# Grouped attention with its queries computed transposed, and the rotation's two parts stacked in 128 rows

## The reference

```
Q = (layernorm(x) @ Wq) -> 16 heads of 64      K, V = ctx @ Wk, ctx @ Wv -> 4 groups of 64
rope(x1, x2) = (x1 * c1 - x2 * s1,  x1 * s2 + x2 * c2)      # halves of 32; position = row
scores = rope(Q) . rope(K) / 8 + rel_pos_bias;  masked
x = x + softmax(scores) @ V -> heads side by side -> @ Wo
```

## Time and profile before

| | us |
|---|---|
| 3 runs, median (lowest, highest) | 1008.42 (1007.82, 1012.86) |
| the profiled execution | 1005.3 |
| its span | 1003.5 |
| TensorE matmul busy | 899.9 (90%) |
| VectorE busy | 669.8 (67%) |
| ScalarE busy | 420.8 (42%) |
| GpSimd busy | 375.3 (37%) |
| grouped attention, first query product to last output | 581.5 to 800.5 |

### The profile page before, as it was taken

The page is one execution under the profiler, slowest core; times in us unless marked ns, Lnnn a source line. Parts: engine busy times, 40 slices in busy tenths (PEclk is TensorE's granted clock), DMA queues, the critical chain, the costliest instruction groups (busy, mean ns, idle before and its releaser), DMA issues. The chain is left out here.

```text
span 1003.5 us, 17466 instructions
## 1 busy us (share of the span) xinstructions
PE 899.9 (90%) x5857; PEld 642.7 (64%) x5864; DVE 669.8 (67%) x1572; ACT 420.8 (42%) x1134; POOL 375.3 (37%) x279
## 2 busy tenths in 40 slices
PE   2899989999889995868899979999999949999997
PEld 2687744444478873744378647777777727778786
DVE  5899968889689988876377698787767531222221
ACT  2566641000146555752455336565655512122222
POOL 1776403333476732506545503333333430111111
PEclk9999999999899997987999999999999969999999
DMA  6100079999400007202356392311110149534200
GB/s 210 59 1 0 1 199 306 319 313 311 170 1 1 0 1 190 87 0 92 112 169 203 91 332 73 112 54 51 51 51 26 43 157 318 190 110 141 93 12 20
DMA packets 87259, 117.17 MB, mean 117 GB/s; under 512 B 12464, under 2 KB 75949, under 8 KB 86781
## 3 DMA queue, kind: packets, MB, share of 16 engines
q1 hardware_dynamic: 77455, 88.15, 29.1%
q10 hardware_dynamic: 4408, 15.46, 4.4%
q0 software_dynamic: 5328, 12.70, 3.5%
HBM read 68.08 MB, written 50.16 MB: 118 GB/s over the span
## 5 line engine op out<-in xcount | busy, mean ns | idle before, releaser
L1016 PE MATMUL psum<-m_W,lnT 128*128 128x512 f32 x256 | 114.2, 598 | 0.7 <-DVE acc L928 0.7
L410 POOL TENSOR_TENSOR prob<-prob,a_rden 128x1232 f32<-128x1232 f32 x30 | 67.5, 2249 | 58.4 <-DVE a_rden L506 58.4
L1016 PEld LDWEIGHTS psum<-m_W,lnT 128*128 128x128 f32 x256 | 47.2, 190 | 59.0 <-issue 56.5
L2907 ACT ACTIVATE prob<-psum,x_b 128x320 f32<-128x320 f32 x64 | 33.7, 527 | 117.1 <-PE psum L2963 117.1
L2574 PE MATMUL psum<-g_VW,pT 128*128 128x256 f32 (+1 forms) x320 | 72.5, 382 | 1.6 <-ACT pT L2461 1.5
L1001 POOL TENSOR_TENSOR m_masked<-m_rel,m_mrow 128x1232 f32<-128x1232 f32 x16 | 41.8, 2614 | 82.9 <-DMA masked_bias<-m_masked 62.0
L2769 POOL DMA_INDIRECT out_x<-x_yt,x_X x20 | 19.8, 991 | 135.3 <-DVE x_yt L2846 135.3
L2574 PEld LDWEIGHTS psum<-g_VW,pT 128*128 128x128 f32 (+1 forms) x320 | 59.5, 190 | 11.2 <-issue 3.7
L2232 POOL TENSOR_TENSOR g_qr<-g_t 128x1024 f32<-128x1024 f32 x15 | 35.4, 2359 | 71.1 <-DVE g_t L2305 71.1
L2239 POOL TENSOR_TENSOR prob<-prob,g_rden 128x1232 f32<-128x1232 f32 x15 | 33.7, 2247 | 67.6 <-DVE g_rden L2340 67.6
L2524 PE MATMUL psum<-g_Wq,lnT 128*128 128x512 f32 x128 | 58.0, 596 | 0.7 <-ACT lnT L2435 0.7
(11 more groups left out here) (464 smaller groups left out, 2235.6 us busy)
## 6 DMA issues: line engine op xcount, KB each, us to landing
routed_rows<-hole SPq DMA_DIRECT2D x8, 2210.0 KB, 33.5
masked_bias<-m_masked ACTq DMA_DIRECT2D x16, 616.0 KB, 7.5
g_bias<-masked_bias SPq DMA_DIRECT2D x16, 616.0 KB, 3.8
m_xb<-routed_rows SPq DMA_DIRECT2D x39, 130.0 KB
m_rel<-in_rel_bias ACTq DMA_DIRECT2D x8, 616.0 KB, 9.6
expert_rows<-hole SPq DMA_DIRECT2D x1, 4680.0 KB, 32.4
g_early_w<-in_L_ffn_w SPq DMA_DIRECT2D x8, 512.0 KB, 4.6
g_early_w<-in_L_ffn_w SPq DMA_DIRECT2D x4, 1024.0 KB, 5.9
```

The costliest lines, as they stand in the source:

```text
L410: nc.gpsimd.tensor_tensor(heads(c.prob[b]), heads(c.prob[b]), rden[b][:, :].unsqueeze(2).to_broadcast([P, H, SK]), ALU.mult).then_inc(norm ...
L1016: last = nt.matmul(c.ps[p][:, :], c.lnT[b][:, k * P:(k + 1) * P], W[:, k, p * 512:(p + 1) * 512], start=(k == 0), stop=(k == KC - 1))
```

## The change

The product is turned round: Wq is now the stationary side and the transposed tile the moving one, so queries arrive with the numbers of two heads on the rows and tokens on the columns. VectorE multiplies them by tables of 64 rows into `turned`, where each head has 128 rows: one half the product with the table "to itself", the other with the table "to the partner". The keys are stored once as they are and once with halves exchanged, one below the other, so one matmul of 128 rows gives a head's scores. GpSimd's sum, the 8 transposes and the 2 copies are gone; scores are 16 matmuls of 77 columns. The rotation of a tile is split around the softmax's shift.

```diff
+        def rope(i, u):
+            q = c.psall[:, q_bank(i) * 512:q_bank(i) * 512 + 1024].rearrange("p (m n) -> p m n", n=P)
+            to = turned[i % 2][:, :].rearrange("p (m u n) -> p m u n", u=2, n=P)
+            n0 = i % HALF * P
+            own, other = slice(u * DH, (u + 1) * DH), slice((1 - u) * DH, (2 - u) * DH)
+            if u == 0:
+                dve.wait_ge(s["q_ps"], i + 1)
+                wait(dve, s["s_ps"], i - 1)
+            for rows_, table in ((own, turn[0]), (other, turn[1])):
+                last = nv.tensor_tensor(to[rows_, :, u, :], q[own, :, :],
+                                        table[own, n0:n0 + P].unsqueeze(1).to_broadcast([DH, HB // 2, P]), ALU.mult)
...
+        def queries(i):
+            pe.wait_ge(s["lnT_ok"], i + 1)
+            if i >= 2:
+                pe.wait_ge(s["roped"], 1 if i == 2 else i)
+            for m in range(HB // 2):
+                to = c.psall[:, q_bank(i) * 512 + m * P:q_bank(i) * 512 + (m + 1) * P]
                 for k in range(KC):
+                    last = nt.matmul(to, Wq[:, k, m * P:(m + 1) * P], c.lnT[i % 2][:, k * P:(k + 1) * P],
+                                     start=(k == 0), stop=(k == KC - 1))
...
+        def scores(t):
+            pe.wait_ge(s["roped"], t + 1)
             wait(pe, s["s_used"], t)
+            for h in range(HB):
+                o = h // HPB * 512 + h % HPB * SK
+                last = nt.matmul(c.psall[:, o:o + SK], turned[t % 2][:, h * P:(h + 1) * P], KB[:, t // HALF, h // G, :],
+                                 start=(h % HPB == 0), stop=(h % HPB == HPB - 1 or h == HB - 1), skip_group_check=True)
```

```diff
+            nv.reduce_max(mx[b][:, halves[0]], p[:, halves[0]], AX, negate=True).then_inc(s["mx_ok"], 1)
             dve.wait_ge(s["s_used"], t + 1)
+            nv.reduce_max(mx[b][:, halves[1]], p[:, halves[1]], AX, negate=True).then_inc(s["mx_ok"], 1)
```

The orders are written anew. VectorE in step t: rope(t+1, 0), shift(t), rope(t+1, 1), the router's work, the residual of tile t-1 (`finished`), the experts' results of one or two tiles (`collect`; groups of statistics are now 0, 1-3, 4-6, 7-10, 11-15), reciprocals (`divisors`). ScalarE and TensorE:

```diff
+        deviation(0)
+        layer_norm(0)
+        lnT_copy(0)
+        deviation(1)
+        na.activation(spare[:, :], c.ones[:, 0:1], ACT.Exp)
+        for i in range(1, 4):
+            layer_norm(i)
+            lnT_copy(i)
+        for t in range(NT):
...
+            if t > 0:
+                pT_copy(t - 1, 0)
+                pT_copy(t - 1, 1)
+            if 2 <= t and t + 3 < NT:
+                layer_norm(t + 3)
+            exps(t, 0, 2)
+            if t > 0:
+                pT_copy(t - 1, 2)
+            exps(t, 2, HB // 2)
+            if t == LOGITS_AT:
+                route(t)
+            exps(t, HB // 2, HB)
...
+        lnT(0)
+        queries(0)
+        lnT(1)
+        queries(1)
+        lnT(2)
+        for t in range(NT + 1):
             banks_read(t)
+            if t < NT:
+                scores(t)
             if t == 0:
+                queries(2)
+                lnT(3)
+            if t == NT - 1:
...
+                pe.wait_ge(s["pT_ok"], (NT - 2) * 3)
+                keep_warm(c, ring[0], 6)
...
+                prob_transpose(t - 1, 0)
+                prob_transpose(t - 1, 1)
...
+                output(t - 1, 0)
+                prob_transpose(t - 1, 2)
+                if t < NT:
+                    route(t)
+                output(t - 1, 1)
+                if 2 <= t and t + 3 < NT:
+                    lnT(t + 3)
+                output(t - 1, 2)
+                back(t)
+                if t + 2 < NT:
+                    queries(t + 2)
+                if t == 1:
+                    lnT(4)
```

More of the change, by code:

```diff
@@ L2224, in _ @@
         ng = nc.gpsimd
[L2226 to L2232, removed]
+        for t in range(NT - 1):
+            b = t % 2
             if t == NT - 2:
@@ L2236, in step @@
                     scatter_tile(c, r, k)
[L2237 to L2245, removed]
+            pool.wait_ge(s["rd_ok"], t + 1)
+            ng.tensor_tensor(heads(c.prob[b]), heads(c.prob[b]),
+                             rden[b][:, :].unsqueeze(2).to_broadcast([P, HB, SK]), ALU.mult).then_inc(s["p_ok"], 1)
+        for k in range(3, HALF):
+            scatter_tile(c, r, k)
     @programs.vector
@@ L2262, in add_experts @@
                 stats = nv.bn_stats(bst_of(c, i), xt(c, tile(i)))
[L2263 removed]
+            if tiles[-1] + 1 in [hi for _, hi in NORM_GROUPS]:
                 chain(stats)
@@ L2330, in residual, with divisors @@
-        def residual(i, b):
+            nv.reduce_max(mx[b][:, halves[1]], p[:, halves[1]], AX, negate=True).then_inc(s["mx_ok"], 1)
+        def divisors(t):
+            b = t % 2
+            wait(dve, s["p_ok"], t - 1)
+            dve.wait_ge(s["exp_ok"], t + 1)
+            nv.reciprocal(rden[b][:, :], den[b][:, :]).then_inc(s["rd_ok"], 1)
+            if t == NT - 1:
+                p = heads(c.prob[b])
+                dve.wait_ge(s["rd_ok"], t + 1)
+                for h in halves:
+                    nv.tensor_tensor(p[:, h], p[:, h], rden[b][:, h].unsqueeze(2).to_broadcast([P, HB // 2, SK]),
+                                     ALU.mult).then_inc(s["p_last"], 1)
@@ L2331, in residual, with finished @@
+        def finished(i):
             dve.wait_ge(s["y_ps"], i + 1)
             nv.tensor_tensor(xt(c, tile(i)), xt(c, tile(i)), bank_y[:, 0:D], ALU.add).then_inc(s["x_ok"], 1)
[L2334 to L2344, removed]
-                                     ALU.mult).then_inc(s["p_last"], 1)
+            dve.wait_ge(s["x_ok"], i + 1)
+            nv.tensor_copy(c.gap[:, i % 2:i % 2 + 1], c.ones[:, 0:1])
+            stats = nv.bn_stats(bst_of(c, i), xt(c, tile(i)))
+            if i + 1 in (HALF, HALF + 4):
+                chain(stats)
+                variance(group_of((i + 1 - HALF) // 4)[1], s["r_ve_ok"])
@@ L2368, in route, with centred @@
                 row_statistics(c, 1)
-            if t == HALF + 7:
-                dve.wait_ge(s["r_back_ps"], 2)
-                first_expert(c, dve, r, 1, c.ps[4][:, 0:2 * P], chain, s["r_lg_read"], 2).then_inc(s["r_oh_ok"], 1)
+        def centred():
+            dve.wait_ge(s["r_sum_ps"], 1)
+            for k in range(KC):
+                nv.scalar_tensor_tensor(out=r.rw[:, k, :], in0=bank_y[:, 0:RW], scalar=-1.0 / D, in1=r.rw[:, k, :],
+                                        op0=ALU.mult, op1=ALU.add).then_inc(s["r_rw_ok"], 1)
         def places(t):
@@ L2500, in step @@
                 na.activation(spare[:, :], c.ones[:, 0:1], ACT.Exp)
-        step(-2, 2)
-        deviation(1)
-        layer_norm(1, 1)
-        for t in range(-1, NT + 1):
-            step(t, t % 4)
+        for u in range(3):
+            pT_copy(NT - 1, u)
         na.activation(spare[:, :], c.ones[:, 0:1], ACT.Sqrt)
@@ L2566, in output @@
-        def output(i, b):
-            if i == 0:
-                pe.wait_ge(s["r_rw_ok"], KC)
-            wait(pe, s["x_ok"], i)
-            for j in range(NB):
-                if j % 4 == 0:
-                    pe.wait_ge(s["pT_ok"], i * 3 + (j // 4 + 1))
-                w = P if j < NB - 1 else LASTB
-                last = nt.matmul(bank_y[:, 0:D], c.pT[b][0:w, j * P:(j + 1) * P], VW[0:w, i // HALF, j, :],
+            if i == NT - 1 and u < 2:
+                pe.wait_ge(s["p_last"], u + 1)
@@ new lines, in prob_transpose @@
+            if u == 0:
+                wait(pe, s["pT_ok"], i * 3)
+            elif u == 1:
+                pe.wait_ge(s["lnT_ok"], min(i + 4, NT))
+            else:
+                pe.wait_ge(s["pT_ok"], i * 3 + 1)
+            for j in range(4 * u, min(4 * u + 4, NB)):
+                w = P if j < NB - 1 else LASTB
+                last = nt.transpose(ring[u % 2][0:w, (j % 4) * P:(j % 4 + 1) * P],
+                                    c.prob[i % 2][:, j * P:j * P + w], c.ident[:, :])
+            last.then_inc(s["pT_ps"], 1)
@@ L2575, in output @@
+        def output(i, u):
+            if u == 0:
+                wait(pe, s["x_ok"], i)
+            pe.wait_ge(s["pT_ok"], i * 3 + (u + 1))
+            for j in range(4 * u, min(4 * u + 4, NB)):
+                w = P if j < NB - 1 else LASTB
+                last = nt.matmul(bank_y[:, 0:D], c.pT[i % 2][0:w, j * P:(j + 1) * P], VW[0:w, i // HALF, j, :],
                                  start=(j == 0), stop=(j == NB - 1))
-            last.then_inc(s["y_ps"], 1)
+            if u == 2:
+                last.then_inc(s["y_ps"], 1)
```

378 lines of the change are left out of this document (148 added, 230 removed).

## The result

The changed kernel is slower. Its median is 1041.18 us (1037.12 to 1042.24, 4 runs) against 1008.49 us (1007.82 to 1012.86) for the kernel before on the same chip: ratio 1.0307, 95% interval 1.0267 to 1.0348. The forecast was 1031 us, its range 1008 to 1043. The profiled execution took 1037.12 us, span 1035.3. By the profiled executions the loss is 31.8 us, where the sum said 24.2.

What follows compares the result with a forecast made beforehand. TensorE was taken to bound the grouped attention, its period rising from 12.46 to 13.46 us. Walks of 20.9 us plus 3.3 for the clock gave 24.2, hence 1031 us; 8-in-10 range 1008 to 1043, own range 1022 to 1040.

Steps and rivals of the forecast that it cites:

- the sum said 24.2: Whole kernel: start 2.7, tiles 2 to 14 10.7, tile 14 2.0, tail 5.5, plus 3.3 for the clock.
- Scores: Each tile's scores: 32 weight loads at 0.113 us make 3.62 us where 2.10 stood, plus 1.52.
- The rival by which the loads hide: Score matmuls issue at 0.067 us, saving 1.48 us a tile: 1008.9 us, or 1001 without waits; chance 0.13.
- loads in series: Rival: load and stream times add up, so scores cost 2.1 us more a tile: 1065 us; chance 0.03.
- ends that cost nothing: Rival: no waits at start, tile 14 and tail, no clock fall; only 10.7 us stay: 1019 us; chance 0.14.
- Query products, transposes, order: Each tile: query products 3.57 us (plus 0.14), query transposes gone (minus 0.88), last two probability transposes later (plus 0.22).
- The margin of 1.3 us: Middle tiles: GpSimd's probabilities ready at 11.7 us (12.2 with two expert tiles), TensorE asks at 13.46: hidden by 1.3 or more.
- first query product to scores 2: Start of the stage: table loads and queue order on ScalarE delay scores 2 from 617.68 to 620.4, plus 2.7 us.
- scores 2 to 14: Tiles 2 to 14: twelve periods of 13.46 us plus router work make 165.4 us against 154.7, plus 10.7.
- scores 14 to 15: Tile 14: scores 15 wait for ScalarE's router copies behind 16 exponentials; 13.5 us against 11.5, plus 2.0.
- scores 15 to the last output's end: Tail: 22.1 us against 16.6, with ScalarE's 16 exponentials and a copy ending at 14.9; plus 5.5.
- The clock: TensorE at half clock after an idle time near 3 us, costing 3.4; one of four counted, 3.3 us.

Runs made afterwards that it cites:

- Splitting and widening the matmuls, each alone: Two runs: kernel before with 154-column score matmuls split into two of 77, ratio 1.0225; changed kernel with eight of 154 for sixteen of 77, 1.0079.
- the widened form: Changed kernel with eight score matmuls of 154 columns a tile for sixteen of 77, half of the scores left out; 1.0079 of the kernel before.
- The run with filler: Changed kernel with 13, 12, 12 and 15 unread warm-up matmuls in TensorE's four idle places; 1.0181 of the kernel before.
- the form with two heads on 128 rows: Kernel before with transposed query product, two heads sharing 128 rows, eight 154-column score matmuls; 1.0231, then 1.0141, 0.9985 and 0.9954 as waits were taken away.
- the last version: Two heads on 128 rows, waits loosened, plus other banks for tile 1's queries and normalized tile, and filler; 0.9954 of the kernel before, 1002.05 us.
- the run before that one: Two heads on 128 rows, two waits loosened, normalized tile's transposes after four output matmuls and its copy ahead of the exponentials; 0.9985 of the kernel before.

## Why the prediction was right, and what was mis-sized

**Scores.** Forecast 3.62 us, measured 3.53: a pitch of 0.110 for each load and not 0.113. Splitting and widening the matmuls, each alone, moved the period by 1.44 us. The rival by which the loads hide is refuted; so is that of loads in series, which wanted about 5.7 us, and that of ends that cost nothing, by the table below. The Trainium skill ("TensorE: Matmul & The Clock Gate", LDWEIGHTS) puts a load at its columns over 1.2 GHz, an estimate of 107 ns for 128; the 0.110 is 3% more.

**Query products, transposes, order.** 3.57 forecast and measured; the last two transposes cost their 0.22. Period forecast 13.46, measured 13.38.

**What should hide, hid, once by luck.** VectorE's 64-row operations take 1.22 us each, the price of 128 rows, as taken, and the rotation is ready 0.67 us before TensorE asks (forecast 0.6). For GpSimd's probabilities the walk was too short. In a step that collects two expert tiles it had them 12.2 us after the end of the scores and TensorE asking at 13.46; they come 13.42 after it, at 653.48, when TensorE is just done with the next scores:

```profile
651.23 2.25 POOL L2229 TENSOR_TENSOR prob<-prob,g_rden 128x1232 f32<-128x1232 f32 x1 [12.16 <-DVE g_rden L2319]
...
653.54 1.09 PE L2552 MATMUL psum<-ident,prob 128*128 128x128 f32 x8
```

The margin of 1.3 us wasn't there; with scores 1.44 us shorter, in the widened form, this step waits 1.36 us.

**Start, tile 14 and tail, without the clock.** The run with filler has all waits but no half clock, so its trace is the walk's test:

| | forecast | with filler | changed kernel |
|---|---|---|---|
| first query product to scores 2 | +2.7 | 39.18 - 36.18 = +3.0 | 41.75: +5.6 |
| scores 2 to 14 | +10.7 | 164.84 - 154.74 = +10.1 | 167.82: +13.1 |
| scores 14 to 15 | +2.0 | 12.99 - 11.51 = +1.5 | 13.00: +1.5 |
| scores 15 to the last output's end | +5.5 | 22.42 - 16.56 = +5.9 | 28.48: +11.9 |
| sum | 20.9 | 20.4 | 32.1 |

The sum of the walks, 20.9, is 0.5 off, in part by luck: two terms are 0.3 and 0.4 too small, two 0.6 and 0.5 too large.

**The clock is the term that was mis-sized.** I had foreseen four idle times of 2.9 to 3.6 us (they are 3.19, 2.97, 2.81 and 3.55), had a row by which one such wait costs 3.4 us, and then counted one of four: 3.3 us. All four are followed by the half level and all but little of it is on the path: 32.1 - 20.4 = 11.7 us by the traces, 12 by the filler's times. The forecast was 8.4 short here; 4 x 3.3 = 13.2 would have given 34.1 for the sum, against 31.8. Outside these rows the stage begins 3.0 us earlier in this execution and what follows it takes 205.8 us in place of 203.0: with 32.1 that makes the 31.8, within the rounding. I did not look for the cause of these two, which nearly cancel and are smaller than the scatter of the runs (5 us).

So the result lies in the stated range near its upper end, and 1 us above the narrower one, 1022 to 1040, which allowed for up to three falls of the clock where there were four.

What stays open is which part of the tail belongs to the exponentials that all sum themselves (sixteen for eight) and which to the halved maximum and new order: no run took these apart.

## What to carry to other kernels

On a TensorE-bound stage, count the stationary loads of a rearrangement before its columns: an f32 matmul of 77 columns cost its load of 128 here (0.110 us) and not its columns, and filling all rows of the array gained nothing because it doubled the loads. When a walk through queues finds a new idle time of some 3 us on a busy TensorE, put down the wait and, behind each one, its own fall of the clock. An operation taken off the critical engine is worth its time only after the waits that it had covered are moved too: the form with two heads on 128 rows went from 2.3% slower to level with the kernel before by a bank and a copy's place, and to 0.5% below it with the first tiles' banks, a last step that is within the scatter.

## What the hardware showed that was not expected

Idle times shorter than the four can be followed by the half level as well: in the last version the idle times ahead of tile 1's scores and tile 0's probabilities are only 1.83 and 1.94 us, with filler between them, and still the next output ran in part at half clock:

```profile
603.40 1.09 PE L2545 MATMUL psum<-ident,prob 128*128 128x128 f32 x8 [1.94 <-POOL prob L2244]
...
605.18 3.40 PE L2558 MATMUL psum<-g_VW,pT 128*128 128x256 f32 x8
```
```profile
605.30:608.30 3.00, 3.00 (x9) 2.37 (x9) 2.96 (x3) 0.44 (x2) 0.79 (x1) 0.51 0.00 0
```

The length of an idle time alone doesn't decide it. In the run before that one (ratio 0.9985) the first three query products take 5.46 or 5.47 us in place of 3.84, behind idle times of 1.3 to 1.7 us with filler between, at a granted clock of 0.83 from 573 to 603 us; in the kernel before, idle times of 1.73 and 1.93 us in the same part of the stage leave the clock at 1.00. What makes the difference stays open.

VectorE's price doesn't fall with the rows: 1.22 to 1.23 us for 1024 elements on 64 rows, from rows 64 to 127 into rows 0 to 63 and the other way, as on 128.
